# Grouped-query attention of a two-layer kernel: query blocks in the order 0, 7, 1, 6, 2, 5, 3, 4, keys and values a group ahead

## The reference, cut to what matters

```python
q = (x @ Wq.T).reshape(b, s, H, HD)      # s 1024, H 32, HD 128
k = (x @ Wk.T).reshape(b, s, HKV, HD)    # HKV 8
v = (x @ Wv.T).reshape(b, s, HKV, HD)
q = _rmsnorm(q, q_norm_w); k = _rmsnorm(k, k_norm_w)
scores = einsum("bkgqd,bksd->bkgqs", q by group, k) / sqrt(HD)
bias = where(rel > 0, -1e30, slopes * rel)          # causal
attn = softmax(scores + bias)
out = einsum("bkgqs,bksd->bkgqd", attn, v) -> (s, H*HD)
return out @ Wo.T
```

## Time and profile before

| | us |
|---|---|
| median of 3 runs | 1687.73 (1662.25 to 1707.97) |
| the profiled execution | 1669.64 |
| its span | 1667.8 |
| from the start of slot 0 to the last slot's end, in that span | 1159.65 |

### The profile page before, as it was taken

One profiled execution on the slowest core, in us unless ns is written; L12 is line 12 of the kernel. 1 busy time (PEld: TensorE's weight loads), 2 busy tenths in 40 slices (PEclk: granted clock), 3 DMA queues, 4 the chain that ended last, 5 costly groups with the idle time before them and its releaser, 6 DMA issues. The chain is left out here.

```text
span 1667.8 us, 26437 instructions
## 1 busy us (share of the span) xinstructions
PE 1475.4 (88%) x7580; PEld 1151.9 (69%) x7580; DVE 1006.4 (60%) x1811; ACT 847.3 (51%) x2152; POOL 658.2 (39%) x926
## 2 busy tenths in 40 slices
PE   4989974699979989997998899799989989989997
PEld 3843322587868768776877787687878778767775
DVE  5575727467657665765766577576667767741322
ACT  3114662366646655655665566465566656642221
POOL 5000005354435444444543454354455445423342
PEclk9975995799989999998999899899999999999998
DMA  4000013101010110101010110101011011032231
GB/s 156 1 1 1 1 35 111 34 14 52 8 60 27 33 40 21 46 14 60 27 33 24 37 37 23 60 18 41 18 41 36 22 39 40 20 101 76 60 117 38
DMA packets 27882, 67.62 MB, mean 41 GB/s; under 512 B 3105, under 2 KB 3233, under 8 KB 27730
## 3 DMA queue, kind: packets, MB, share of 16 engines
q1 hardware_dynamic: 27730, 65.79, 12.6%
HBM read 55.82 MB, written 9.96 MB: 39 GB/s over the span
## 5 line engine op out<-in xcount | busy, mean ns | idle before, releaser
L1217 DVE CUSTOM_DVE_ANT_0 PB<-S,REL,SLC 128x128 f32<-128x128 f32 (+7 forms) x256 | 207.3, 812 | 118.9 <-PE S L1373 118.9
L604 POOL TENSOR_SCALAR PB<-PB,RI 128x128 f32<-128x128 f32 (+7 forms) x256 | 240.9, 941 | 49.3 <-POOL RI L603 46.1
L834 ACT ACTIVATE PB<-PB,NM 128x128 f32<-128x128 f32 (+7 forms) x256 | 197.8, 773 | 115.9 <-DVE NM L1217 113.8
L876 ACT ACTIVATE R<-T 128x512 fp32r<-128x512 f32 x288 | 169.7, 595 | 135.6 <-PE T L1652 133.4
L603 POOL TENSOR_TENSOR RI<-SM,C 128x1 f32<-128x1 f32 x256 | 140.1, 547 | 241.2 <-ACT PB L834 240.2
L1125 DVE TENSOR_TENSOR R<-T,R 128x512 fp32r<-128x512 f32 x288 | 196.5, 689 | 62.2 <-ACT R L876 56.1
L1652 PE MATMUL T<-C,PB 128*128 128x128 f32 x1152 | 174.4, 277 | 30.1 <-DVE R L1125 12.8
L1371 PE MATMUL S<-R 128*128 128x512 f32 (+2 forms) x488 | 183.3, 376 | 9.7 <-DVE NM L1217 4.5
L1652 PEld LDWEIGHTS T<-C,PB 128*128 128x128 f32 x1152 | 135.0, 141 | 60.5 <-DVE R L1125 24.2
L1373 PE MATMUL S<-R 128*128 128x512 f32 (+2 forms) x488 | 174.8, 358 | 0.0
L1372 PE MATMUL S<-R 128*128 128x512 f32 (+2 forms) x488 | 174.0, 357 | 0.0
(11 more groups left out here) (176 smaller groups left out, 3449.8 us busy)
## 6 DMA issues: line engine op xcount, KB each, us to landing
RAW<-w SPq DMA_DIRECT2D x36, 384.0 KB, 3.6
PB<-dequantised SPq DMA_DIRECT2D x20, 512.0 KB, 3.6
RAW<-w SPq DMA_DIRECT2D x38, 256.0 KB, 2.6
DQ<-codes SPq DMA_DIRECT2D x16, 352.0 KB, 3.3
DQ<-absmax SPq DMA_DIRECT2D x16, 352.0 KB, 2.9
dequantised<-DQ SPq DMA_DIRECT2D x16, 352.0 KB, 2.3
PB<-x SPq DMA_DIRECT2D x16, 256.0 KB, 3.2
x_scratch<-PB SPq DMA_DIRECT2D x8, 256.0 KB, 3.1
```

What stands on the lines that cost most here:

```text
L604: e.tensor_scalar(PB[:, m % 2, a, 0:L], PB[:, m % 2, a, 0:L], RI[:, k:k + 1], scale, ALU.mult, ALU.mult).then_inc(probs_ready, 1)
L834: e.activation(PB[:, m % 2, a, 0:L], PB[:, m % 2, a, 0:L], ACT.Exp, scale=-1.0, bias=NM[:, k:k + 1], accum_out=SM[:, k:k + 1]).then_inc(ex ...
L876: e.activation(r(PT + AT[i, ("PV", kb)] % 3 * 1024, 512), T[AT[known, it] % 2][:, :], ACT.Copy).then_inc(t_act, 1)
L1217: e.tensor_tensor_reduce(out=PB[:, m % 2, a, 0:L], in0=bank[:, 0:L], in1=REL[:, TOK - L:TOK], scale=SLC[:, a:a + 1], scalar=3.0e38, op0=AL ...
```

## The change

The blocks of a group are taken in the order 0, 7, 1, 6, 2, 5, 3, 4. Since block 7 then needs all keys early, keys and values are projected a group ahead, into a second set of buffers (K2, beside the old place in R), and the prologue projects all eight key and value blocks of group 0. Weights are cut otherwise: four chunks of 512 for the queries (in the slot of block 5), two of 2x256 for keys and values (in the slot of block 4), four of 512 for the output (in the slot of block 0). `WO` moves from the fourth head's to the second head's place in all slots but the first of a group. The loop has three passes over sixteen slots. Scores are no longer padded to 256 columns. PB, the probabilities, shrinks to 512 and 1024 columns per head for even and odd slots. The core of the diff:

```diff
-T_BASE = T_PRO + 6
+ORDER = (0, 7, 1, 6, 2, 5, 3, 4)
+def block_of(n):
+    return ORDER[n % NT]
...
-    i = n % NT
-    nk = i + 1
+    j = n % NT
+    nk = block_of(n) + 1
...
-    put("V")
+    put("V", when=0 < n <= STEPS - NT)
     for a in range(4):
-        if a == 3:
-            put("WO", when=i != 0)
+        if a == 1:
+            put("WO", when=j != 0)
         if a == 0:
             put("PQ", when=s2)
         put(("S", a), when=s1)
         if a == 0:
-            put("PKV", when=s2)
+            put("PKV", when=kv)
...
         put(("EX", a), when=s1)
-        put(("CH", a + 3), when=i == 0 and a > 0)
-        put(("CH", a), when=n < STEPS - NT and i == 5)
+        put(("CH", "W", a - 1), when=j == 0 and a > 0)
+        put(("CH", "Q", a), when=n < STEPS - NT and j == 5)
+        put(("CH", "K", a - 1), when=n < STEPS - 2 * NT and j == 7 and a in (1, 2))
...
-    put(("CH", 7), when=i == 0)
+    put(("CH", "W", 3), when=j == 0)
...
+PRO = [("KV", 0), ("KV", 1)]
+for _b in range(2, NT):
+    PRO += [("KV", _b), ("KT", _b - 2)]
+    if _b in (3, 4):
+        PRO.append(("QT", _b - 3))
+    if _b in (2, 3):
+        PRO.append(("PQ", _b - 2))
+PRO += [("KT", NT - 2), ("KT", NT - 1)]
...
-    with eng.Fori(0, HKV - 1) as g:
+    with eng.Fori(0, LOOPS - 1) as g:
-        for i in range(1, NT + 1):
+        for i in range(1, LOOP + 1):
...
-                    w = min(512, max(256, L - c))
-                    last = mm3(bank[:, c:c + w], r(q, P), r(q + 512, P), r(KTR + c, w), r(KTR + TOK + c, w), True, True)
+                    w = min(512, L - c)
+                    last = mm3(bank[:, c:c + w], r(q, P), r(q + 512, P), kv(m // NT, c, w), kv(m // NT, TOK + c, w),
+                               True, True)
```

More of the change, by code:

```diff
@@ L197 @@
 EX_BASE = EX_PRO + 4
-P_PER, V_PER = 56, 3
+P_PER, V_PER = 112, 6
+C_PRO = {("K", 0, 0): 0, ("K", 0, 1): 1, ("Q", 0, 0): 2, ("Q", 0, 1): 3, ("Q", 0, 2): 4, ("Q", 0, 3): 5,
+         ("K", 1, 0): 6, ("K", 1, 1): 7}
 def _tables():
     t, s, w, pv = T_BASE, S_BASE, W_BASE, PV_BASE
+    c = len(C_PRO)
+    sq = 8
     at = {}
+    for k in range(4):
+        at[-3, ("CH", "Q", k)] = C_PRO["Q", 0, k]
+    for k in range(2):
+        at[-1, ("CH", "K", k)] = C_PRO["K", 1, k]
     for n in range(STEPS):
@@ L283, in slots @@
     for t, s in zip(tallies, start):
-        t.base, t.n = 0, s + (HKV - 1) * t.per
-    for i in range(1, NT):
-        slot(HKV - 1, i)
+        t.base, t.n = 0, s + (LOOPS - 1) * t.per
+    for i in range(1, LOOP):
+        slot(LOOPS - 1, i)
 def program(nc, x, w0, w1, codes, absmax, lora, consts, rows, rel, out):
@@ L342, in program @@
         CODES = DQ[:, 0, :].bitcast(I32)
-        Y_AT = (6, 7, 14, 15)
+        Y1 = [K2F[:, tt * D:(tt + 1) * D] for tt in range(4)]
         IDENT = C[:, C_ID:C_ID + P]
@@ L515, in slot @@
                 if jj == 0:
                     load_codes(g, i)
[L517 to L534, removed]
+                if known == 0 and isinstance(g, int):
+                    w1_first("K", 1, 0)
+                    w1_first("K", 1, 1)
@@ new lines, in slot @@
+                if j == 0:
+                    for k in range(4):
+                        w1_next("W", g, i, k)
+                if not isinstance(g, int) or known < STEPS - NT:
+                    if j == 2:
+                        w1_next("Q", g, i + 3, 0)
+                        w1_next("Q", g, i + 3, 1)
+                    if j == 5:
+                        w1_next("Q", g, i, 2)
+                        w1_next("Q", g, i, 3)
+                if (not isinstance(g, int) or known < STEPS - 2 * NT) and j == 6:
+                    w1_next("K", g, i + 1, 0)
+                    w1_next("K", g, i + 1, 1)
@@ L849, in lines @@
                 for ln in todo.get((jj, part), ()):
[L850 removed]
+                    chunk = g * 4 + i // 4
                     to = {0: 1, 4: 2}.get(ln, 3)
@@ L1237, in combine @@
                 jj = i % 4
-                chunk = g * 2 + i // 4
-                if jj == 0 and part == 0 and not (isinstance(g, int) and 8 * g + i == 0):
+                chunk = g * 4 + i // 4
+                if jj == 0 and part == 0 and not (isinstance(g, int) and LOOP * g + i == 0):
                     dve.wait_ge(in_absmax, chunk * 16)
```

505 lines of the change are left out of this document (325 added, 180 removed).

## The result

The changed kernel takes 1776.2 us (median of 4 runs, 1760.2 to 1805.0), the kernel before 1675.8 (4 runs, 1662.3 to 1708.0): ratio 1.065, 95% interval 1.052 to 1.078. Forecast were 1733 and +45 us; the profiled execution is 106.9 us longer (1776.56 against 1669.64). The direction was right, the size less than half of it.

What follows compares the result with a forecast made beforehand. TensorE was the engine to watch, with chunk slots paced by a DVE and ScalarE chain. Slots +33 and prologue +12 gave +45 us on the median 1687.7, so 1733; range 1640 to 1780.

Steps and rivals of the forecast that it cites:

- chain of rows 6: DVE and ScalarE alternate: maximum, exponential, copy, low half, next maximum; slots with chunks go at its pace.
- walk of block 0's slot: Step-by-step timing of block 0's slot: ends at 20.3 us, TensorE waiting 3.0 for QN, then 3.1.
- Rival (a): Slots: balance works, each comes near its TensorE work; 98 us less, 1590 on the median; chance 0.25.
- early projection: WO placed early leaves QN uncovered; slots of blocks 1 to 3 come 0.8 to 2.3 us over their work.
- walks' sum: The eight slots of a pass, each timed step by step, sum to 149.0 us against 142.6.
- half-clock stretches: Gaps in the slots of blocks 0 and 4 lower TensorE's clock: 3 us a pass, bounds 0 and 6.
- groups 0 to 5: Slots of the first six groups: 152 us a pass each, 912 in all.
- group 7: Last group, no keys or values projected and no next queries in its last two slots: 126 us.
- branches: Loop's end: two branches back, between 0 and 11.8 us, taken as 8.
- The prologue: Before the slots: eight key and value blocks through two T banks, some 34 to 40 us, +12.
- narrow matmuls: Score matmuls under 256 columns: -0.3 to +2.6 us a pass, taken as 0.
- Rival (c): Slots slower: half clock in three per pass, narrow matmuls at the high bound; +85, 1773; chance 0.1.

Runs made afterwards that it cites:

- a_swap: Changed kernel with ScalarE copying the weight chunk before the head's exponential instead of after it; ratio 1.031 to the kernel before.
- b_swap: Kernel before with ScalarE copying the weight chunk before the head's exponential instead of after it; ratio 0.976 to the kernel before.
- a_wo4: Changed kernel with the output projection back from the second head's place to the fourth's; ratio 1.002 to the kernel before.
- a_order_wo4: Changed kernel with the output projection at the fourth head's place and the milder block order 0,4,1,5,2,6,3,7; ratio 1.003 to the kernel before.
- a_qn1: Changed kernel with QN, the scaling of the queries, asked for at the second head instead of the third in blocks 0 to 3; ratio 1.071 to the kernel before.
- b_wo5: Kernel before with the output projection behind the fourth head's scores instead of ahead of them; ratio 1.017 to the kernel before.

## Why the prediction went wrong where it did

**The path held.** The chain of rows 6 is real: a_swap and b_swap took out one link of it and got back 40 and 33 us. The walk of block 0's slot named its waits: 2.51 us for QN and 2.34 for the low half (walked 3.0 and 3.1), DVE idle 1.83 ahead of the chunk (1.9). Block 5's slot is 21.1 (20.6). Rival (a), that every slot comes near to its work, fails in either order: a_wo4 has TensorE busy 133.7 of 146.5, a_order_wo4 133.7 of 143.4. For interleaving stretches with different limits, of which the Trainium skill (Perfetto Trace Analysis, Optimization Strategy) says that it may help, the orders by themselves show no gain here (1.002 and 1.003).

**The step that failed is the early projection, which I counted "only through the walks".** The prediction gave it 0.8 to 2.3 us in three slots and put the rest on chunks beside wide scores. The runs turn that round: the order with everything else costs nothing clear of noise (1.002), the place of the projection costs all (1.077 alone; 10.7 us a group, and 88 us over all slots, in the changed kernel). Against a_wo4 it costs 1.4, 2.2 and 1.2 us in the slots of blocks 1, 2 and 3, as I had it; another 5.9 us a group fall in the others, 3.0 of them in block 4's, where I put no price on it. I never walked the same slots with the projection at the fourth place, which would have set a price on this edit by itself.

The walks' sum also missed two terms. Against 149.0 a group there are 157.2. The half-clock stretches of a group come to 10.2 us (6.8 from block 0's slot into block 7's, 3.4 around 653.5 in block 4's), which cost at most 5.1, where I took 3; the row of the first:

```profile
515.30:522.10 6.80, 4.06 (x12) 3.10 (x13) 4.54 (x9) 5.32 (x11) 3.79 (x4) 0.50 0.19 64
```

And six waits of 0.5 us for a bank of the ring, 3.1 in all, five of them of the projection, stood in no walk: I had followed DVE's queue, but not who still held the bank that the moved projection writes to. That 149.0 + 5.1 + 3.1 is 157.2 is luck, for it does not close slot by slot. The slots of blocks 1, 6, 2, 5 and 3 ran at full clock and took 93.7 us where the walks had 88.9, with 2.0 of ring waits between them; in what way the other 2.8 came stays open. Those of blocks 0, 7 and 4 took 63.5 instead of 60.1, less than the clock and the ring at their full price.

**The terms one by one** (slots, forecast +33, measured +83.9, so 51 missing): groups 0 to 5, 157.2 instead of 152, 31; group 6, 153.6 instead of 147, 7; group 7, 134.0 instead of 126, 8; branches, 163.6 less 157.2 for each of two, 12.8 instead of 8, 5. For group 7 my own terms don't give 126: 147 less 8 x 1.44 and two query projections of 2.72 is 130. The prologue came as forecast, 36.6 us against 37. Outside the forecast stand the 13 us of the first layer, and the last part of the span was 2 shorter. 45 + 51 + 13 - 2 is the 107 of the profile.

**Why the order comes out at nothing.** By a_wo4 against before: the longer groups (146.5 instead of 142.6, less in the first and the seventh) cost 25 us; two slow branches of 3.9 us in place of five give back 21; group 7, now without keys and values to project, is 8 shorter, the prologue 12 longer, the tail 2 shorter: +6, which is 0.4% and within the interval. So the walks were right that the new order's slots are longer, and the milder order takes back 3.1 of the 3.9, 2.6 of it in block 0's slot, where 640 columns stand beside the chunks instead of 1024; fewer branches and the shorter group 7 pay for most of the rest. The narrow matmuls (0.06 to 0.11 us apart) are at the forecast's low bound and cost nothing, as taken.

Rival (c), 1773, came nearest to the time. One part of its way is there: half clock touches three slots of a group, at 0.87, 0.97 and 0.92 where it named 0.85, for at most 5.1 us where it took 6. The other part, dear narrow matmuls, is not, and the early projection stands in it no more than in the forecast.

## What to carry over

When an edit moves a long item of the busiest engine, walk the slot twice, with the item at the old and at the new place, and follow three things: which scores it now delays, whose queue its consumer joins, and who still holds the buffer that it writes to. An engine with some 10% to spare can still lose 7% by issuing work in an order that starves a two-engine chain; what that chain feeds on goes first, bulk work goes where the chain has enough ahead of it, though not so late that its buffer comes back late. And before blaming the name in a wait, move that one item: where the wait only changes its name, the whole chain is late.

## What the runs showed of the hardware

The first layer took another time in every profiled execution: 285.0 to 318.4 us in twelve and 335.1 in a_qn1's, the longest, over kernels of both kinds; at 126 us they still stand within 2.1 us of one another. Each program was profiled once, so that one and the same program's first layer moves is not shown; but 13 executions of the kernel before on one chip took 1652.8 to 1697.1 us, at granted clocks from 0.945 down to 0.910. The slowest (a_qn1) and one of the fastest (b_wo5), from 98.8 us to the first projection:

```profile
98.80:335.10 236.30, 196.46 (x726) 77.95 (x724) 118.16 (x163) 80.78 (x153) 21.34 (x28) 0.52 0.08 24
```

```profile
98.80:288.40 189.60, 147.09 (x731) 62.40 (x729) 118.73 (x165) 80.41 (x154) 22.80 (x28) 0.76 0.11 32
```

DVE does the same work in both (118.2 and 118.7 us); TensorE is granted 0.52 or 0.76 of its clock. What tips it stays open. It is as large as many of the effects here, so the parts of the change had to be compared from the end of the first layer on.

Taken branches cost TensorE 3.3 to 5.4 us in 41 of 46 cases over the thirteen traces. The five others, of 0.23 to 0.24 us, were all in the shorter loop of eight slots (of 30), none in the loop of sixteen (of 16). The Trainium skill (Runtime: NRT & Kernel Launch, Instruction fetch mechanics) says that a taken branch whose target is outside the two pages held has to fetch it first; the 41 slow ones fit that, and nothing in the traces explains the five.
